# A small clearing on GpSimd ahead of each node load, slot scatter and second-layer gather of a four-layer graph network

## The reference

```python
h = relu(layernorm(x)); x = x + L0(h)   # 4 heads of attention: exp(leaky(s_src + s_dst)), sums over edges, elu
h = relu(layernorm(x)); x = x + L1(h)   # weighted midpoint in hyperbolic space
h = relu(layernorm(x)); x = x + L2(h)   # 8 heads of attention of 64, then one of 128
h = relu(layernorm(x)); x = x + L3(h)   # three hypergraph convolutions with batch norm

# L1, the layer whose gathers the change touches:
x_hyp = expmap0(h); gamma = 2 / clip(1 - sum(x_hyp * x_hyp))
num = segment_sum(weight[:, None] * (gamma * x_hyp)[dst], src)
den = segment_sum(weight * (gamma - 1)[dst], src)
out = logmap0(mobius_scalar_mul(0.5, num / den))
```

## Time and profile before

| what | us |
|---|---|
| median of 3 runs (5017.53 to 5023.84) | 5017.77 |
| the profiled execution | 5050.38 |
| its span, first to last instruction | 5048.3 |
| busy: DVE / POOL / PE / ACT | 2841.8 / 2034.5 / 1680.4 / 1641.0 |
| place_edges, from GpSimd's first to VectorE's last instruction | 243 to 424 |
| layer norm with scatters | 428 to 534 |
| scores_once, up to the stage after it | 544 to 1125 |
| second layer's loop | 2281 to 3288 |

### The profile page before, as it was taken

One profiled execution on the slowest core, in us unless ns is written; L12 is line 12 of the kernel. 1 busy time (PEld: TensorE's weight loads), 2 busy tenths in 40 slices (PEclk: granted clock), 3 DMA queues, 4 the chain that ended last, 5 costly groups with the idle time before them and its releaser, 6 DMA issues. The chain is left out here.

```text
span 5048.3 us, 46860 instructions
## 1 busy us (share of the span) xinstructions
PE 1680.4 (33%) x10711; PEld 946.3 (19%) x10711; DVE 2841.8 (56%) x4778; ACT 1641.0 (33%) x4317; POOL 2034.5 (40%) x1847
## 2 busy tenths in 40 slices
PE   4133200100000000001544433522222237899989
PEld 3022100100000000000111110111111127644444
DVE  5728567781677779871333332564877875722131
ACT  1312301110556657001544443513444454310010
POOL 0055778806777720026133444126776742000000
PEclk6566555555555555555656565665555568999999
DMA  3000000005666620002011122216877826578856
GB/s 121 18 12 1 3 1 1 1 0 158 171 184 182 184 57 0 0 16 51 18 41 44 52 58 56 57 70 197 260 240 226 252 76 183 196 271 274 271 168 210
DMA packets 215383, 553.41 MB, mean 110 GB/s; under 512 B 46177, under 2 KB 112411, under 8 KB 214404
## 3 DMA queue, kind: packets, MB, share of 16 engines
q0 software_dynamic: 99984, 272.83, 19.8%
q1 hardware_dynamic: 115188, 278.18, 16.2%
HBM read 485.70 MB, written 65.20 MB: 109 GB/s over the span
## 5 line engine op out<-in xcount | busy, mean ns | idle before, releaser
L1187 POOL DMA_INDIRECT blend_got<-rec,blend_slot x416 | 396.0, 952 | 532.0 <-DVEq L1230 389.3
L912 POOL DMA_INDIRECT table<-edges_record,edges_place x391 | 517.9, 1325 | 139.3 <-issue 123.2
L2707 PE MATMUL fourth_bank<-fourth_tile,fourth_z 128*128 128x512 f16 (+1 forms) x2800 | 559.9, 361 | 19.9 <-DVEq L2868 10.1
L2069 POOL DMA_INDIRECT heads_got<-rec,heads_slot x416 | 469.3, 1128 | 177.5 <-issue 124.6
L247 PE MATMUL blend_count<-blend_mov,blend_stat 128*128 x980 | 358.6, 451 | 545.9 <-issue 439.8
L1623 POOL DMA_INDIRECT sum_got<-rec,sum_slot x416 | 457.0, 1099 | 157.2 <-issue 124.2
L1239 DVE TENSOR_SCALAR blend_mov<-built_iota_low,built_low 128x800 f16 x490 | 213.1, 435 | 506.4 <-issue 330.2
L1697 DVE TENSOR_TENSOR rounds_y<-rounds_y,sum_got 128x516 f32 x416 | 290.9, 699 | 125.0 <-issue 33.5
L1267 ACT ACTIVATE blend_gap<-built_iota_ten,built_offset 128x128 f32 x490 | 196.8, 402 | 486.0 <-issue 395.0
L203 PE MATMUL edges_p_key<-kept_ident,edges_key_row 128*128 128x128 f32 x4 | 1.1, 428 | 1035.5 <-DVEq L170 1035.5
L2707 PEld LDWEIGHTS fourth_bank<-fourth_tile,fourth_z 128*128 128x128 f16 x2800 | 261.8, 99 | 311.7 <-issue 15.2
(11 more groups left out here) (666 smaller groups left out, 4403.0 us busy)
## 6 DMA issues: line engine op xcount, KB each, us to landing
fourth_tile<-cs SPq DMA_DIRECT2D x100, 800.0 KB, 4.5
fourth_tile<-ct SPq DMA_DIRECT2D x100, 800.0 KB, 4.5
ct<-blend_cst SPq DMA_DIRECT2D x20, 1000.0 KB
heads_counts<-ct SPq DMA_DIRECT2D x25, 800.0 KB
cs<-heads_flipped SPq DMA_DIRECT2D x25, 800.0 KB
attend_cnt<-ct SPq DMA_DIRECT2D x50, 256.0 KB
sort_low_wide<-low SPq DMA_DIRECT2D x4, 3136.0 KB
attend_cnt<-ct SPq DMA_DIRECT2D x25, 288.0 KB
```

Of the source, the lines that this page charges most:

```text
L912: pool.indirect_dma_start(table, bass.IndirectOffsetOnAxis(ap=K["place"][0:lanes, t:t + 1], axis=0), K["record"][0:lanes, t, :], None).the ...
L1187: pool.indirect_dma_start(got[:, buf, r, :], None, rec_dram, bass.IndirectOffsetOnAxis(ap=slot[:, t:t + 1], axis=0)).then_inc(gathered[t % ...
L2069: pool.indirect_dma_start(got[:, buf, r, :], None, rec_dram, bass.IndirectOffsetOnAxis(ap=slot[:, t:t + 1], axis=0)).then_inc(gathered[buf ...
L2707: last = pe.matmul(bank[m][:, 0:w], z2[s % 2][:, k, part, :], tile[:, n % RING, at:at + w], start=(k == 0 and part == 0), stop=(k == NB - ...
```

## The change

GpSimd gets a tile `rest` of 128 x 112 float32 (kept for the whole kernel) that nobody reads. Ahead of each of the 25 node loads, 391 slot scatters and 416 gathers of the second layer it now clears that tile with a memset. Each memset raises a semaphore, and each but the first of a Pause waits for the one before. The gathers of the first and third layer and the other indirect DMAs are as before.

```diff
+REST = 112
+class Pause:
+    def __init__(self, tile, sem):
+        self.tile, self.sem, self.n = tile, sem, 0
+    def __call__(self, pool):
+        if self.n:
+            pool.wait_ge(self.sem, self.n)
+        pool.memset(self.tile, 0.0).then_inc(self.sem, 1)
+        self.n += 1
...
-def put_records(pool, K, table, first, end, listed):
+def put_records(pool, K, table, first, end, listed, pause):
...
             pool.wait_ge(listed[t % IN_FLIGHT], 16 * (t // IN_FLIGHT))
+        pause(pool)
         pool.indirect_dma_start(table, bass.IndirectOffsetOnAxis(ap=K["place"][0:lanes, t:t + 1], axis=0),
...
                     pool.wait_ge(gathered[b % IN_FLIGHT], 16 * (b // IN_FLIGHT))
+                pause(pool)
                 pool.indirect_dma_start(x[:, b, :], None, x_dram, bass.IndirectOffsetOnAxis(ap=K["order"][:, b:b + 1], axis=0),
...
+    pause = Pause(K["rest"][:, :], c.sem("rested"))
...
                         pool.wait_ge(gathered[t % IN_FLIGHT], 16 * (t // IN_FLIGHT))
+                    pause(pool)
                     pool.indirect_dma_start(got[:, buf, r, :], None, rec_dram,
...
+             "rest": c.sb("rest", [P, REST])}
...
+            listing = Ctx(nc, inner, "table")
+            listed, pause = listing.lanes("listed"), Pause(K["rest"][:, :], listing.sem("rested"))
```

More of the change, by code:

```diff
@@ L437, in _, with scores_once @@
             act.activation(root[:, :], var[:, :], ACT.Sqrt).then_inc(a, 1)
-def scores_once(nc, K, h, w_col, a_col, s_col, d_col, table, listed):
+def scores_once(nc, K, h, w_col, a_col, s_col, d_col, table, listed, pause):
     heads = w_col.shape[1]
@@ L469, in _ @@
         def _(pool):
-            put_records(pool, K, table, PUT_BEFORE, ET, listed)
+            put_records(pool, K, table, PUT_BEFORE, ET, listed, pause)
             wait_landed(pool, listed, ET)
@@ L928, in blank_table, with place_edges @@
         end_pass(nc)
-def place_edges(nc, K, x_dram, table, listed):
+def place_edges(nc, K, x_dram, table, listed, pause):
     EQUAL, FOUND = 3, 3
@@ L968, in _ @@
                 pool.wait_ge(placed, g + 1)
-                put_records(pool, K, table, g * GROUP_E, (g + 1) * GROUP_E, listed)
+                put_records(pool, K, table, g * GROUP_E, (g + 1) * GROUP_E, listed, pause)
             wait_landed(pool, gathered, NB)
@@ L1846, in _, with first_layer @@
             lift(3)
-def first_layer(nc, K, table, listed, rec_dram, w_dram, a_dram):
+def first_layer(nc, K, table, listed, pause, rec_dram, w_dram, a_dram):
     heads = w_dram.shape[0]
@@ L1861, in first_layer @@
             w_all, w_col, a_col = ci.sb("w_all", [P, heads, D + 1]), ci.sb("w_col", [P, heads]), ci.sb("a_col", [P, heads, 2])
-            layer_norm_once(nc, K, h, "norm0", beside=lambda pool: put_records(pool, K, table, PUT_EARLY, PUT_BEFORE, listed))
+            layer_norm_once(nc, K, h, "norm0", beside=lambda pool: put_records(pool, K, table, PUT_EARLY, PUT_BEFORE, listed, pause))
             kept = ci.sem("kept")
@@ L1870, in _ @@
                     sp.wait_ge(kept, 48)
-            scores_once(nc, K, h, w_col, a_col, s_col, d_col, table, listed)
+            scores_once(nc, K, h, w_col, a_col, s_col, d_col, table, listed, pause)
             store_records(nc, K, h, w_all, d_col, rec_dram)
@@ L1889, in first_layer, with sort_edges @@
             finish_once(nc, K, y)
-def sort_edges(nc, K, stack, src, dst, weight, low_dram, row_dram, x_dram, table, listed):
+def sort_edges(nc, K, stack, src, dst, weight, low_dram, row_dram, x_dram, table, listed, pause):
     tiles = GROUPS_E * GROUP_E
@@ L1909, in sort_edges @@
         blank_table(nc, K, table)
-        place_edges(nc, K, x_dram, table, listed)
+        place_edges(nc, K, x_dram, table, listed, pause)
     spread_parts(nc, K, "reach", K["reach"][:, :].unsqueeze(1), K["reach_rows"][:, :].unsqueeze(1))
@@ L3030, in gnn_kernel @@
         K = {"x": c.sb("x", [P, NB, D]), "pad": c.sb("pad", [P, NB]), "zero": c.sb("zero", [P, 512], BF16),
-             "ident": c.sb("ident", [P, P]), "out_deg": c.sb("out_deg", [P, NB]), "inv_in": c.sb("inv_in", [P, NB])}
+             "ident": c.sb("ident", [P, P]), "out_deg": c.sb("out_deg", [P, NB]), "inv_in": c.sb("inv_in", [P, NB]),
+             "rest": c.sb("rest", [P, REST])}
         load_nodes(nc, K, x)
         with ExitStack() as inner:
-            listed = Ctx(nc, inner, "table").lanes("listed")
-            sort_edges(nc, K, inner, src, dst, edge_weight, low, key, x, table, listed)
+            listing = Ctx(nc, inner, "table")
+            listed, pause = listing.lanes("listed"), Pause(K["rest"][:, :], listing.sem("rested"))
+            sort_edges(nc, K, inner, src, dst, edge_weight, low, key, x, table, listed, pause)
             end_layer(nc)
-            first_layer(nc, K, table, listed, rec, l0_w, l0_a)
+            first_layer(nc, K, table, listed, pause, rec, l0_w, l0_a)
             second_layer(nc, K, src, dst, ranges, table, rec1, ct)
```

## The result

The changed kernel took 4893.25 us in the median of four runs (4880.91 to 4894.14) where the kernel before took 5017.89: a ratio of 0.9745 (95% interval 0.9733 to 0.9756), 125 us faster. The profiled execution spans 4892.1 us and took 4894.1. The forecast had 4690; the sign was right, the gain well under half of it.

A forecast was written before the change was run, and what follows sets the result against it. GpSimd's dense indirect DMAs, slowing other engines' instruction issue, were taken to bound the edited stages. Terms -57 + 15 - 36 - 247 = -325 us from the 5017.8 us median gave 4690 us; range a little under 4556 to 5150, the forecast's own 4550 to 4820.

The forecast's parts named there:

- the size of a clearing: On GpSimd's queue each clearing adds +0.35 us, making the period 1.60 us for gathers and 1.62 for scatters.
- rival 3: On GpSimd's queue the clearing fits in the 0.30 us gap after each DMA, so nothing moves: 5018 us; chance 0.08.
- place_edges: Stage with node loads and scatters: TensorE at the free rate ends at 330, GpSimd at 367 instead of 423.7: -57 us.
- layer norm: Layer norm beside scatters: GpSimd is last there, so 54 clearings, less some hidden ones, cost +15 us.
- scores_once: Scores beside scatters: VectorE's slow stretches vanish (81 us), GpSimd becomes the last at 1088: -36 us.
- second layer's loop: Second layer's gathers and tiles: starvation ends and GpSimd becomes the bound, 760 us against 1007: -247 us.
- The diagnosis: In the edited stages GpSimd's regular, dense indirect DMAs slow the other engines' instruction issue, more than any wait for data.
- the point from starved to free: Beside GpSimd's DMA streams, engines go from starved to free near an average period of 1.4 to 1.5 us.
- A clearing beside VectorE: In the loop, clearings held up by VectorE's tile comparison cost 0.1 us a gather: 4730 instead of 4690 us.
- my sentence that a slower GpSimd costs nothing in the loop: Second layer: GpSimd waits 389.3 us for VectorE's buffers, so by that view a slower GpSimd costs nothing.
- Rival 1: place_edges, scores_once and the loop: an even 1.6 us period still starves the others, +158 us, 5176 us; chance 0.22.
- Rival 2: GpSimd's stream too slow (0.6 us a clearing) or relief only partial, in the loop above all: 4896 us; chance 0.15.

The follow-up runs named there:

- e2_two: The changed kernel with two clearings of 112 columns instead of one ahead of each DMA; 4715.1 us, 0.9394 of the kernel before.
- e4: The changed kernel with clearings of 8 columns instead of 112 everywhere; 4986.3 us, 0.9922 of the kernel before.
- g1: The changed kernel with two clearings of 8 columns ahead of each DMA, on a chip with starvation; 4870.1 us, 0.9625 of the kernel before.
- e8: The kernel before, without clearings, with second-layer gathers of 64 rows from the fifth set on; 4373.2 us where the kernel before took 4379.0.
- i2: The changed kernel itself once more, where the kernel before took 4378.5 us; 4469.7 us, 1.0213.
- g3: The kernel before, without clearings, with second-layer gathers of 64 rows from the fifth set on, on a chip with starvation; 5076.2 us, 1.0015.
- e5: The changed kernel with two clearings in place_edges and the second layer's loop, one elsewhere; 4587.0 us (1.0475), rerun on a chip with starvation 4690.1 us (0.9263).

## Why the prediction was wrong

**The step that failed is the size of a clearing.** For its cost I took +0.35 us, the middle of +0.19 and +0.49, and put the case that it slips into the gap outside the forecast, as rival 3. It slips in for the most part: +0.07 (+0.13 by the mean interval in bursts). The earlier trace rows gave its length rightly (0.19 forecast, 0.20 measured at rest); what I had no row for, and priced too high, was what the 0.30 us gap does around it. It is not a fixed cost after each instruction: behind a clearing it is 0.17.

**The rest of the chain was right for place_edges and the loop, and e2_two shows it**, because two clearings add 0.31 us, nearly what I had assumed for one (stages against those of the kernel before on A, in the profiled executions; times by medians):

| term | forecast | e2_two | after |
|---|---|---|---|
| place_edges | -57 | -43 | -2 |
| layer norm | +15 | +13 | +3 |
| scores_once | -36 | +6 | -59 |
| second layer's loop | -247 | -290 | -77 |
| time, us | 4690 | 4715 | 4893 |

- That 4715 lies so near 4690 is in part luck: place_edges is 14 us and scores_once 42 us worse than forecast, the loop 43 us better.
- The diagnosis (GpSimd's dense stream slows the issue of the others, wider spacing frees them) holds on chips A, B and C for place_edges and the loop. For VectorE in scores_once it doesn't: that was the lockstep, which even e4's clearings dissolve at the same usual interval.
- *place_edges*: TensorE was to be done at 330, and was at 330 on D; in e2_two it ended at 349, as 1.59 us between scatters don't free it wholly, and GpSimd at 375 (forecast 367). With one clearing it had next to no relief.
- *scores_once*: VectorE was forecast to end at 1043 and ended at 1039: the 81 us of slow stretches did vanish, for another reason than spacing. GpSimd's last scatter ended at 1060 instead of 1088 because a clearing costs less, so this term beat its forecast. In e2_two the scatters took 36 us more than I had worked out for them.
- *The loop*: the point from starved to free was placed at an average of 1.4 to 1.5 us, by the slow stretch of scores_once (1.40) on one side. That reading was wrong, as 1.40 was made by the lockstep and the earlier trace rows have VectorE free at 38 scatters in 48 us just before it; that the place still came out near the truth was luck. g1 (0.45 tiles a us at 1.38) and e2 (0.68 at 1.56, GpSimd the bound) bracket it: in the loop there is no point but a slope, and at 1.32 the change stands low on it. In the forecast the loop was to be GpSimd's; it is so in e2_two (728 us against 760), and not in the changed kernel, where 266.3 us of waits for VectorE remain.
- *A clearing beside VectorE*: the estimate of 0.1 us a gather for clearings held up by the tile comparison was too high. In the changed kernel's loop a clearing that starts during a comparison takes 0.30 us and the others 0.21, and 79 of 412 do, so it is 0.02 us a gather. In scores_once, beside VectorE instructions with two inputs, a clearing takes 0.21 as elsewhere.

**The rivals.** Rival 1 (an even stream starves the others however wide it is) fell: e2's even 1.56 leaves the loop to GpSimd, and g1's even 1.93 leaves TensorE its full rate. At 1.59 it was right by a third for TensorE in place_edges. Rival 2 named the time, 4896, and in its second clause the kind of thing that happened (a burst rate half way up from 0.26 to 0.74; 0.375 is a quarter of the way), but its first clause, a clearing of 0.6 us, was the opposite of the truth. Rival 3's mechanism, the clearing in the gap, was mostly true and its conclusion, no change, was not: the clearing is worth 2.5% here, some of it in scores_once, where its length hardly counts. I treated 0.07 and 0 as one.

**What the trace of one chip could not tell.** I read the starvation as a property of the kernel. It is one of the kernel on some chips (or in some state of a chip that lasts; only C was seen twice): the change is 2.5% faster on A, 2.0% on C, and 2.1% slower on F, where my sentence that a slower GpSimd costs nothing in the loop is wrong too. In e8 on D GpSimd waits 13.1 us for VectorE's buffers where before on A waits 389.3, in i2 on F not at all: there its stream bounds the loop.

Beside this stands the Trainium skill, Runtime: NRT & Kernel Launch, "Instruction fetch mechanics", by which a crossing into a new block is mostly hidden. On D it looks so. On C the engines stall, but not by fetching more. Instruction queues of g3 on C (packets, MB, share of the DMA engines' span); the same program on D, e8, has the same two rows:

```profile
q8 instruction: 82, 1.34, 0.1%
q14 instruction: 129, 1.06, 0.1%
```

What in the chip or its surroundings makes the difference stays open; no run here can show it.

## What to carry to other kernels

An instruction put between two others costs what it adds to the interval, not its length: look for the gap it can sit in, and price that case as the first, not as a rival. Where a quantity has to pass a point for a gain (here the interval), test a series of sizes before trusting one, and read it stage by stage: g1's 1017 matmuls looked like half a relief and were a full one beside one stream and none beside the other. Before a stall's period is taken for its condition, look at what the two engines did just before it set in: 1.40 us was made by the lockstep, 1.28 was what went before. And run a change that rests on a stall of "issue", with no one waited for, on more than one chip: the same edit was worth -2.5% and +2.1%, and e5's edit, 0.9263 on C, was 1.0475 on D.

## What the hardware showed that I had not expected

- The same program took 5018 to 5066 us on two or three chips and 4378 to 4379 on three others, 640 to 690 us apart; most of it in stages beside dense streams of GpSimd's indirect DMAs (the loop alone 429, scores_once 103, place_edges 71 between the profiles of before on A and e8 on D).
- Where it starves, GpSimd's DMA stream slows TensorE, VectorE and ScalarE the more, the closer its DMAs follow each other. The loop of all three makes 0.26 tiles a us at 1.25 us, 0.45 at 1.38, and 0.68 at 1.56, where GpSimd is the bound. TensorE in place_edges makes 2.3 matmuls a us at 1.28 and at 1.41, 13.6 at 1.59 and 20.2 at 1.93, and 14.5 when 1.31 and 2.50 alternate. Half the rows in each DMA change nothing (0.25 at 1.21).
- Two VectorE instructions of 0.57 us fit beside each scatter 1.28 us apart, or only one, in lockstep with the scatter's end, for 48 to 63 us on end in the same execution; a clearing of 0.13 us between the scatters is enough to keep nearly all of this away.
- The 0.30 us between two indirect DMAs takes in a 0.20 us clearing for +0.07.
- The first burst of 104 gathers needs 136 us and makes 136 tiles on D; with clearings it makes 40 tiles in 146 us on A.
- In place_edges TensorE's clock went with the relief: granted 0.53, the level of 1.2 GHz and a little more, with 237 matmuls in 97.6 us, and 1.00, the level of 2.4 GHz, with 1648.
